# The way into a state-space loop: SiLU by exponential and logarithm, batches 0 to 2 ahead, TensorE's order written by hand

## The chip, the cores and the metric

The kernel runs as one program on one core of a Trainium2 chip. The metric is the device time of an execution in microseconds, from the first to the last instruction of the core. The engines are written as the profile writes them: PE is TensorE (PEld its weight loads), ACT is ScalarE, DVE is VectorE, POOL is GpSimd, SP the engine that issues DMAs. They run side by side and meet at semaphores. Each engine works through its own instructions in the order in which they are written.

## The reference

Two layers of a small network over `x` (4 batches, 128 tokens, 128 channels) and a context (4 batches, 2048 keys), all float32. The part that the change touches is the first layer's state-space branch and the two attentions on either side of it:

```python
x = x + L0_xattn(layernorm(x), ctx)      # attention over every 16th key, 16 heads of 8
x = x + L0_attn(layernorm(x))            # the state-space branch, below
...                                      # quantised feed-forward, gated attention over the context
x = x + L1_attn(layernorm(x))            # self-attention with a relative bias
...                                      # quantised feed-forward

xi, res = split(x @ W_in)                # 256 channels each
u = silu(conv4(xi) + conv_b)             # causal convolution with 4 taps
dbc = u @ W_x                            # 8 + 16 + 16 values of each token
delta = softplus(dbc[:8] @ W_dt + b_dt)
h = exp(delta * A) * h + delta * B * u   # over the tokens, for 16 states
y = (sum over states of h * C + u * D) * silu(res)
return y @ W_out
```

## The kernel before, in words

Channels or tokens lie on the 128 partitions, and the 512 tokens of the four batches along the free dimension. Every engine's program is written out by hand, so the order of the code is the order on the engine, and semaphores named after tensors (`S["u"]`, `S["dt_ps"]`) hold the engines together. A helper `mm` issues every matmul, so that most of PE's matmuls bear one line (L1076). A product in float32 shows as two matmul instructions in the trace.

Both attentions run through the function `attention(ph)`, which each engine has in its own version: `ph` 0 is the cross-attention of layer 0, `ph` 1 the self-attention of layer 1. Step `t` handles the scores of one batch and head group (16 in all, four for each batch), and the later stages of a batch `b` come due at step `4 * b + stage`, by a table of constants: INVERSE 6, INVERSE_T 7, VALUES 8 (`pv`, then `spread_ps`), SCALE 9 (DVE writes `attn_T`), PROJECT 10 (PE multiplies `attn_T`), ADD 11 (DVE makes the new `x` and its moments), RSTD 11, NORM 12, TURN 13. Within a step PE does: scores, the turned probabilities of step t-2, values and their scale, projection. DVE does: `neg_max` (the maximum of the scores), the copy of turned probabilities, `attn_T`, sum and moments, norm, reciprocal. ACT does the four exponentials, and then `o_T`, the copy of `pv`. The last steps (16 to 25) hold only the stages of batches 2 and 3.

After the cross-attention comes the way into the state loop. The convolution is folded into the input projection: for each of four taps one matmul with `w_tap` (the input weights times the tap) on a shifted view of `xn_pad`. The tokens are cut into three groups, batches 0 and 1, batch 2, batch 3 (`SSM_GROUPS`). `channels` issues the convolutions (`part` 0 and 1, the two halves of 128 channels) and the gate's product; the first group's are spread over steps 17 to 25 of the attention by the table `CHANNELS`. ACT takes SiLU of each straight out of PSUM (`channel_inputs`, `gates`). For that it loads the table set of SiLU before (L492), and the set of exponential and logarithm again behind (L528). Then for all 512 tokens at once: PE makes `dbc_ps`; ACT copies its first 8 rows (`dt_low`) and rounds 96 rows to bf16 (`bc_parts`); DVE takes the two remainders of that rounding (L862, L863), so that three bf16 parts stand for one float32 value; PE makes `dt_ps`; ACT takes the absolute value, exponential and logarithm (L532 to L536), DVE the positive part (L867); their sum is `delta` (L873), and `du` is `delta * u`, for the first half on DVE (L877), for the second on POOL (L384). During the remainders PE runs 16 matmuls on ones, whose result nobody reads (`keep_warm`).

The loop has 32 steps k, one for each state n and half. DVE makes `drive` (L884, `du` times the row of B that PE spreads over the partitions) and runs the scan (L900); ACT makes `decay` (L556) and copies the spread row of C; POOL multiplies the state by C (`read`, L392), and PE adds that up in PSUM (`y`) on top of the product with `skip`. Behind it DVE multiplies with the gate (L905). POOL quantises the weights of the feed-forwards in three instructions each (L375 to L377), the first three ahead of the loop, two behind.

## Time and profile before

| | |
|---|---|
| time, median of 3 runs | 279.73 us (277.42 to 280.04) |
| span of the profiled execution | 278.8 us |
| PE busy | 209.7 us (75%) |
| DVE busy | 205.7 us (74%) |
| ACT busy | 151.6 us (54%) |
| POOL busy | 74.6 us (27%) |
| table loads of ACT on the way in | 2, each 1.28 us |
| first scan of the state loop | 85.55 us from the start |

The profiled execution is one of its own, and only its span is given, no time beside it; the span lies between the lowest and the highest of the three runs. The busy shares are means over stages with different limits, so they don't say what a stage waits for: the rows further down, cut by stage, do.

### The profile page before, as it was taken

What the parts mean: (1) busy time and instruction counts of PE and PEld (TensorE: products, weight loads), DVE (VectorE), ACT (ScalarE), POOL (GpSimd) and SP (SyncE); (2) the same over time, 40 slices, a digit from 0 to 9 for tenths busy, and PEclk for the clock granted to TensorE, in tenths of its full rate; (3) what the DMA queues carried; (4) which work ended last, traced back from release to release, by engine and by line L of the source; (5) the groups of instructions that cost most, each with busy time, mean ns of one, the idle gap of its engine ahead of it and who ended that gap; (6) DMA issues with size and microseconds to landing.
All of it is one profiled execution on the core that took longest, in us unless ns stands there. A gap on an engine that the chain in (4) does not pass through costs nothing.

```text
span 278.8 us, 4790 instructions
## 1 busy us (share of the span) xinstructions
PE 209.7 (75%) x1557; PEld 141.2 (51%) x1559; DVE 205.7 (74%) x585; ACT 151.6 (54%) x510; POOL 74.6 (27%) x73
## 2 busy tenths in 40 slices
PE   6896988898786977777762577999996699973313
PEld 4475877676752322222131354777785688851102
DVE  6358648873069999999957975767767499985675
ACT  4357659643685555555317773245336689853420
POOL 5013000049305777777794010000001000001000
PEclk9688999999979799999996899999999899997555
DMA  7999700068830000000000005000000000000001
GB/s 225 429 393 414 317 2 2 0 74 93 94 45 0 1 0 1 0 0 0 2 1 0 1 0 150 2 0 2 0 1 0 4 1 2 0 4 0 4 0 38
DMA packets 6745, 16.06 MB, mean 58 GB/s; under 512 B 320, under 2 KB 5056, under 8 KB 5696
## 3 DMA queue, kind: packets, MB, share of 16 engines
q1 hardware_dynamic: 6720, 15.75, 19.7%
q8 instruction: 13, 0.21, 0.3%
q14 instruction: 12, 0.10, 0.1%
HBM read 13.39 MB, written 2.35 MB: 56 GB/s over the span
## 4 chain that ended last, share of the span: by engine, by line
PE 38%; DVE 24%; POOL 13%; issue 12%; ACT 9%; DMA 2%; POOLq 0%; SPq 0%; another core or an unknown queue 0%; DVEq 0%; ACTq 0%
PE bank L1076 31%; POOL region L392 13%; ACT probs L477 3%; PE bank L1416 3%; DVE region L775 2%; DVE region L758 2%; DMA ctx_T_sb<-ctx_T 2%; PE bank L1189 2%; DVE neg_max L753 1%; DVE xn L685 1%; DVE stats L680 1%; PE bank L1093 1%; DVE ext L1040 1%; DVE ext L1041 1%; DVE v_heads L698 1%
## 5 line engine op out<-in xcount | busy, mean ns | idle before, releaser
L1076 PE MATMUL bank<-region,early_sb 128*128 128x512 f32 x64 | 36.8, 661 | 11.8 <-POOL region L392 11.6
L392 POOL TENSOR_TENSOR region<-region 128x512 f32<-128x512 f32 x32 | 40.5, 1268 | 14.5 <-DVE region L900 14.5
L900 DVE TENSOR_TENSOR_SCAN region<-region,bank 128x512 f32<-128x512 f32 x32 | 38.7, 1211 | 0.0
L1076 PE MATMUL bank<-k_groups,region 128*128 128x128 f32 x256 | 35.7, 285 | 1.2 <-ACT k_groups L459 1.2
L1076 PEld LDWEIGHTS bank<-k_groups,region 128*128 128x128 f32 x256 | 32.2, 198 | 3.2 <-ACT k_groups L459 1.8
L361 POOL TENSOR_TENSOR xb<-x,rows_sb 128x512 f32<-128x512 f32 x3 | 3.8, 1261 | 101.0 <-DVE x L790 43.2
L477 ACT ACTIVATE probs<-bank,neg_max 128x128 f32<-128x128 f32 x64 | 22.6, 367 | 12.9 <-DVE neg_max L753 12.5
L1076 PE MATMUL bank<-ctx_T_sb,region 128*32 128x128 f32 (+1 forms) x288 | 26.8, 345 | 3.4 <-DMA ctx_T_sb<-ctx_T 2.2
L477 ACT ACTIVATE probs<-region,neg_max 128x128 f32<-128x128 f32 x64 | 24.9, 390 | 5.7 <-DVE neg_max L758 5.5
L1076 PEld LDWEIGHTS bank<-region,early_sb 128*128 128x128 f32 x64 | 10.1, 195 | 33.2 <-POOL region L392 32.6
L775 DVE COPY region<-bank 128x512 f32<-128x512 f32 x32 | 21.8, 682 | 5.6 <-PE bank L1189 5.6
L411 ACT ACTIVATE lnv<-mv,eps_col 128x1 f32<-128x1 f32 x24 | 7.0, 291 | 33.7 <-DVE mv L681 33.6
L542 ACT ACTIVATE region<-bank 128x512 f32<-128x512 f32 x16 | 9.5, 595 | 24.2 <-POOL region L392 24.2
L1189 PE MATMUL bank<-early_sb,probs 128*128 128x128 f32 x128 | 20.7, 287 | 1.5 <-ACT probs L477 1.5
L884 DVE TENSOR_TENSOR bank<-region,bank 128x512 f32<-128x512 f32 x32 | 21.6, 676 | 0.0
L556 ACT ACTIVATE region<-region,a_neg 128x508 f32<-128x508 f32 x32 | 21.1, 708 | 0.0
L758 DVE CUSTOM_DVE_ANT_0 region<-bank,region 128x128 f32<-128x128 f32 x64 | 14.5, 282 | 5.7 <-PE bank L1076 5.7
L1189 PEld LDWEIGHTS bank<-early_sb,probs 128*128 128x128 f32 x128 | 15.2, 146 | 3.5 <-ACT probs L477 2.1
L1007 DVE COPY region<-bank 128x512 f32<-128x512 f32 x16 | 10.9, 686 | 8.1 <-PE bank L1416 8.1
L1076 PEld LDWEIGHTS bank<-region,ctx_sb 128*128 128x128 f32 x128 | 15.4, 192 | 2.9 <-issue 2.9
L1076 PEld LDWEIGHTS bank<-ctx_T_sb,region 128*32 128x32 f32 (+1 forms) x288 | 12.6, 132 | 7.7 <-issue 4.5
L1076 PE MATMUL bank<-region,ctx_sb 128*128 128x128 f32 x128 | 15.6, 275 | 0.0
(198 smaller groups left out, 410.1 us busy)
## 6 DMA issues: line engine op xcount, KB each, us to landing
ctx_sb<-ctx SPq DMA_DIRECT2D x4, 1024.0 KB, 24.5
ctx_T_sb<-ctx_T SPq DMA_DIRECT2D x3, 1024.0 KB, 10.5
late_sb<-late SPq DMA_DIRECT2D x1, 2416.0 KB, 18.4
bias_scratch<-bias_vec SPq DMA_DIRECT2D x1, 2040.0 KB, 24.7
ctx_T_sb<-ctx_T SPq DMA_DIRECT2D x2, 512.0 KB, 6.2
region<-bias_scratch SPq DMA_DIRECT2D x1, 1024.0 KB, 5.7
early_sb<-early SPq DMA_DIRECT2D x1, 512.0 KB, 3.7
region<-taps SPq DMA_DIRECT2D x1, 512.0 KB, 18.9
```

The lines of the kernel that those rows point to most:

```text
L392: done(pool.tensor_tensor(read[:, k % 3, :], state[:, k % 3, :], c_sb[:, n % 2, :], ALU.mult), "read")
L477: ins = act.activation(probs[:, w % 4, j, :], src[:, j, :], ACT.Exp, bias=neg_max[:, w % 4, j:j + 1], scale=1.0 if ph == 0 else -1.0, accu ...
L542: done(act.activation(c_sb[:, n % 2, :], bank[2][:, :], ACT.Copy), "c_sb")
L556: done(act.activation(dst, src, ACT.Exp, scale=a_neg[:, hf, n:n + 1]), "decay")
L758: ins = dve.tensor_tensor_reduce(neg_biased[:, t % 3, j, :], src[:, j, :], rel_bias[:, HG * g + j, :], -1.0, HIGHEST, ALU.add, ALU.min, ne ...
L775: done(dve.tensor_copy(probs_T[:, w % (2 * NG)].rearrange("p h k -> p (h k)"), bank[3 + w % 2][:, :]), "probs_T_sb")
L884: done(dve.tensor_tensor(bank[3 + k % 3][:, :], du[:, hf, :], bank[n % 2][:, :], ALU.mult), "drive")
L900: done(dve.tensor_tensor_scan(state[:, k % 3, :], decay[:, k % NDA, :], bank[3 + k % 3][:, :], 0.0, ALU.mult, ALU.add), "state")
L1007: done(dve.tensor_copy(p2_T[:, w % 4].rearrange("p c q -> p (c q)"), bank[4 + w % 2][:, :]), "p2T_sb")
L1076: return pe.matmul(dst, lhsT, rhs, start=start, stop=stop)
L1189: ins = pe.transpose(bank[3 + w % 2][:, j * P:j * P + P], probs[:, w % 4, j, :], ident)
L1416: ins = pe.transpose(bank[4 + w % 2][:, c * P:c * P + P], p2[:, b % 2, g, c * P:c * P + P], ident)
```

## The change

- `u` and the gate no longer use the SiLU table. DVE takes the convolution with its bias from PSUM, clamped at -80, into `du` (`clamped`), and ACT makes the sigmoid in three steps of one table set, exp(-x), ln(1 + that), exp(-that) (`sigmoids`); POOL (pieces 0 and 1) and DVE (piece 2) multiply. Both table loads go.
- The gate is only clamped on the way in (two halves for batches 0 to 2, one for batch 3). Its six sigmoid steps stand in the state loop on ACT, at k = 6, 8, ... 16, and DVE multiplies them in behind the last scan.
- What was done for 512 tokens at once is done in pieces: `dbc`, the low rank copy, the remainders, `dt_ps`, the logarithm and `delta` for batches 0 to 2 (384 columns, first half), then for batch 3 (128 columns, both halves), then batches 0 to 2 of the second half. The positive part and the sum are one instruction (`stepped`), and the bias has one of its own (`biased`).
- The attention's loop ends at step 16 for `ph` 0, and the rest is written by hand on PE, ACT and DVE with the convolutions between. The copies of the turned `xn` of batches 2 and 3 move from ACT to DVE.
- The table of stages changes for both attentions: PROJECT 10 to 9, ADD and RSTD 11 to 10, NORM 12 to 11; in a step DVE writes `attn_T` ahead of the copy of turned probabilities.
- The 16 matmuls on ones go. The third weight of POOL is quantised behind the loop. `skip` is made at the start. The last `x` shares its memory with the third.

```diff
-INVERSE, INVERSE_T, VALUES, SCALE, PROJECT, ADD, RSTD, NORM, TURN = 6, 7, 8, 9, 10, 11, 11, 12, 13
+INVERSE, INVERSE_T, VALUES, SCALE, PROJECT, ADD, RSTD, NORM, TURN = 6, 7, 8, 9, 9, 10, 10, 11, 13
+STEPS = 4 * NB, NG * (NB - 1) + NORM + 1
-FILLS = {"early_in": 20, "bc_parts": 16, "hidden": 12, "hidden_rest": 12, "swiglu_out": 4}
+FILLS = {"early_in": 20, "hidden": 12, "hidden_rest": 12, "swiglu_out": 4}
+PIECES = [(0, 2), (2, 3), (3, 4)]
+FIRST = 3 * P
+GATE_STEPS = (6, 8, 10, 12, 14, 16)
...
# ACT
+            copy_xn_T(1, 1)
+            heads_out(2)
+            rsqrt_var(1, 2)
+            heads_out(3)
+            rsqrt_var(1, 3)
+            sigmoids(0)
+            sigmoids(1)
+            sigmoids(2)
+            low_rank(0, 3, slice(0, FIRST))
+            log_terms(0, slice(0, 1), slice(0, FIRST))
+            low_rank(1, 4, slice(FIRST, T))
+            log_terms(1, slice(0, DH), slice(FIRST, T))
+            log_terms(2, slice(1, 2), slice(0, FIRST))
...
+            def log_terms(i, hfs, cols):
+                act.wait_ge(S["dt_sum"], i + 1)
+                link(act.activation(sp[:, hfs, cols], delta[:, hfs, cols], ACT.Abs))
+                link(act.activation(sp[:, hfs, cols], sp[:, hfs, cols], ACT.Exp, scale=-1.0))
+                done(act.activation(sp[:, hfs, cols], sp[:, hfs, cols], ACT.Ln, bias=1.0), "sp_exp")
...
# DVE
+            clamped(2)
...
+            done(dve.tensor_tensor(u[:, :, piece(2)], du[:, :, piece(2)], sig[:, :, piece(2)], ALU.mult), "u_last")
+            split(0, 3, slice(0, FIRST))
+            biased(0, 1, slice(0, 1), slice(0, FIRST))
+            split(1, 4, slice(FIRST, T))
+            biased(1, 6, slice(0, DH), slice(FIRST, T))
+            stepped(0, slice(0, 1), slice(0, FIRST))
...
+            stepped(1, slice(0, DH), slice(FIRST, T))
...
+            biased(2, 2, slice(1, 2), slice(0, FIRST))
...
             drive(0)
+            stepped(2, slice(1, 2), slice(0, FIRST))
...
# PE
+            project(0, 3)
+            convolve(0, 1, range(2, CONV))
+            turn_xn(1, 1, 2)
+            convolve(1, 0)
+            convolve(1, 1)
+            turn_xn(1, 1, 3)
+            pe.wait_ge(S["attn"], 4)
+            gates(0, 0, 3, bank[5][:, 0:FIRST])
+            done(gates(1, 0, 3, bank[7][:, 0:FIRST]), "gates_ps")
+            convolve(2, 0)
+            convolve(2, 1)
+            gates(0, 3, 4, bank[0][:, 2 * P:3 * P])
+            done(gates(1, 3, 4, bank[0][:, 3 * P:4 * P]), "gates_ps")
```

ACT between the last SiLU and the first decay of the loop. Before, it stands so:

```order
L451 ACTIVATE region<-bank 128x2x128
L524 ACTIVATE region<-early_sb,cols_sb 128x128 x2
L526 ACTIVATE region<-bank 8x512
L527 ACTIVATE bc_parts<-bank 96x512
L528 ACT_TABLE_LOAD
L532 ACTIVATE region<-bank,cols_sb 128x512 x2
L535 ACTIVATE region<-region 128x512
L536 ACTIVATE region<-region 128x512
```

In the changed kernel, from the last step of the last sigmoid (three more logarithm steps on 384 columns follow ahead of the first decay):

```order
L456 ACTIVATE region<-region 128x2x128
L462 ACTIVATE region<-bank 8x384
L463 ACTIVATE bc_parts<-bank 96x384
L468 ACTIVATE region<-region 128x384
L469 ACTIVATE region<-region 128x384
L470 ACTIVATE region<-region 128x384
L462 ACTIVATE region<-bank 8x128
L463 ACTIVATE bc_parts<-bank 96x128
L468 ACTIVATE region<-region 128x2x128
L469 ACTIVATE region<-region 128x2x128
L470 ACTIVATE region<-region 128x2x128
```

One pair of copies and one set of logarithm steps has become two pairs and three sets, which alternate; the second pair of copies (L462, L463 on 128 columns) stands behind the first set's logarithm.

DVE at the same place. Before:

```order
L862 TENSOR_TENSOR region<-bank,bc_parts 64x512
L863 CAST bc_parts<-region 64x512
L862 TENSOR_TENSOR region<-region,bc_parts 32x512
L863 CAST bc_parts<-region 32x512
L867 TENSOR_SCALAR region<-bank,cols_sb 128x512 x2
L873 TENSOR_TENSOR region<-region 128x512
L877 TENSOR_TENSOR region<-region 128x512
```

In the changed kernel:

```order
L908 TENSOR_TENSOR region<-bank,bc_parts 64x384
L909 CAST bc_parts<-region 64x384
L908 TENSOR_TENSOR region<-region,bc_parts 32x384
L909 CAST bc_parts<-region 32x384
L918 TENSOR_SCALAR region<-bank,cols_sb 128x384
L908 TENSOR_TENSOR region<-bank,bc_parts 64x128
L909 CAST bc_parts<-region 64x128
L908 TENSOR_TENSOR region<-region,bc_parts 32x128
L909 CAST bc_parts<-region 32x128
L918 TENSOR_SCALAR region<-bank,cols_sb 128x128 x2
L925 SCALAR_TENSOR_TENSOR region<-region 128x384
L959 TENSOR_TENSOR region<-region 128x384
```

The remainders and the bias come once for 384 and once for 128 columns, and the first `delta` (L925) stands behind both.

PE in the self-attention, from the values of batch 0 on. Before:

```order
L1076 MATMUL bank5<-region,v_heads 32x128 x16
L1076 MATMUL bank7<-inv_T,cols_sb 128x128
L1076 MATMUL bank0<-k_groups,region 128x128 x4
L1189 MATMUL bank4<-early_sb,probs 128x128 x4
L1076 MATMUL bank1<-k_groups,region 128x128 x4
L1189 MATMUL bank3<-early_sb,probs 128x128 x4
L1076 MATMUL bank5<-late_sb,attn_T 128x128
L1076 MATMUL bank2<-k_groups,region 128x128 x4
```

In the changed kernel:

```order
L1166 MATMUL bank5<-region,v_heads 32x128 x16
L1166 MATMUL bank7<-inv_T,cols_sb 128x128
L1166 MATMUL bank0<-k_groups,region 128x128 x4
L1254 MATMUL bank4<-early_sb,probs 128x128 x4
L1166 MATMUL bank5<-late_sb,attn_T 128x128
L1166 MATMUL bank1<-k_groups,region 128x128 x4
L1254 MATMUL bank3<-early_sb,probs 128x128 x4
L1166 MATMUL bank2<-k_groups,region 128x128 x4
```

The projection of `attn_T` has moved ahead of the scores of step 10 (those into bank1) and of the turned probabilities behind them.

## Rows read from the trace of the kernel before

**Rows 1.** The page: shares of the chain by line.

```profile
PE bank L1076 31%; POOL region L392 13%; ACT probs L477 3%; PE bank L1416 3%; DVE region L775 2%; DVE region L758 2%; DMA ctx_T_sb<-ctx_T 2%; PE bank L1189 2%; DVE neg_max L753 1%; DVE xn L685 1%; DVE stats L680 1%; PE bank L1093 1%; DVE ext L1040 1%; DVE ext L1041 1%; DVE v_heads L698 1%
```

**Rows 2.** Windows: stretch, us; busy PE, PEld, DVE, ACT, POOL; PE clock; DMA, GB/s.

```profile
57.40:74.90 17.50, 15.77 (x150) 13.20 (x150) 6.28 (x22) 9.21 (x31) 12.38 (x9) 1.00 0.84 93
...
78.90:85.50 6.60, 6.10 (x25) 3.31 (x24) 6.27 (x10) 6.50 (x12) 0.63 (x1) 0.74 0.12 16
85.50:139.70 54.20, 42.49 (x92) 12.66 (x90) 54.17 (x64) 27.07 (x46) 39.68 (x32) 0.97 0.00 1
222.60:249.80 27.20, 24.74 (x261) 21.33 (x259) 25.92 (x152) 22.98 (x111) 0.00 (x0) 0.98 0.01 2
```

**Rows 3.** The chain of waits in order of time, 57 to 90 us.

```profile
69.89 5.00 PE bank L1076 x41
74.89 1.84 issue
...
82.76 0.70 DVE region L873
```

**Rows 4.** Timeline, ACT on the way in: start, us, instruction, idle before.

```profile
69.13 1.28 ACT L492 ACT_TABLE_LOAD   x1
...
70.59 0.83 ACT L444 ACTIVATE region<-bank,cols_sb 128x256 f32<-128x256 f32 x2
...
78.92 1.28 ACT L528 ACT_TABLE_LOAD   x1
...
81.37 0.63 ACT L535 ACTIVATE region<-region 128x512 f32<-128x512 f32 x1
...
83.75 0.70 ACT L556 ACTIVATE region<-region,a_neg 128x508 f32<-128x508 f32 x1
```

**Rows 5.** Timeline, DVE from the remainders to the first scans.

```profile
78.94 0.68 DVE L862 TENSOR_TENSOR region<-bank,bc_parts 64x512 f32<-64x512 f32 x1 [9.43 <-ACT bc_parts L527]
...
79.65 0.42 DVE L863 CAST bc_parts<-region 64x512 bf16<-64x512 f32 x1
...
85.55 1.22 DVE L900 TENSOR_TENSOR_SCAN region<-region,bank 128x512 f32<-128x512 f32 x1
...
87.86 1.21 DVE L900 TENSOR_TENSOR_SCAN region<-region,bank 128x512 f32<-128x512 f32 x1
```

**Rows 6.** Timeline: a convolution on PE, POOL's product, PE's skip products.

```profile
60.84 3.72 PE L1076 MATMUL bank<-region 128*128 128x256 f32 x16 [0.37 <-ACT region L419]
...
84.87 1.27 POOL L384 TENSOR_TENSOR region<-region 128x512 f32<-128x512 f32 x1 [12.55 <-DVE region L873]
...
85.22 1.88 PE L1076 MATMUL bank<-region 128*128 128x512 f32 x4
```

**Rows 7.** Windows of one us: columns as in rows 2, granted PE clock third from last.

```profile
82.00:83.00 1.00, 1.00 (x7) 0.67 (x6) 0.92 (x3) 0.97 (x2) 0.00 (x0) 0.50 0.00 0
...
84.00:85.00 1.00, 0.50 (x4) 0.02 (x2) 0.96 (x3) 1.00 (x3) 0.13 (x1) 1.00 0.00 0
...
91.00:92.00 1.00, 1.00 (x2) 0.15 (x1) 1.00 (x2) 1.00 (x3) 1.00 (x1) 0.50 0.00 0
```

**Rows 8.** Timeline, DVE: the last two scans and the gate's product.

```profile
137.41 2.33 DVE L900 TENSOR_TENSOR_SCAN region<-region,bank 128x512 f32<-128x512 f32 x2
...
141.25 0.69 DVE L905 TENSOR_TENSOR region<-bank,region 128x512 f32<-128x512 f32 x1 [1.52 <-PE bank L1076]
```

**Rows 9.** Timeline of the self-attention, engine by engine: PE, ACT, then DVE.

```profile
233.63 1.06 PE L1076 MATMUL bank<-k_groups,region 128*128 128x128 f32 x8
...
234.10 0.28 ACT L488 ACTIVATE o_T<-bank 128x128 f32<-128x128 f32 x1
...
235.04 0.28 DVE L758 CUSTOM_DVE_ANT_0 region<-bank,region 128x128 f32<-128x128 f32 x1
...
242.81 0.29 DVE L758 CUSTOM_DVE_ANT_0 region<-bank,region 128x128 f32<-128x128 f32 x1
...
252.90 0.29 DVE L790 TENSOR_TENSOR x<-bank,xb 128x128 f32<-128x128 f32 x1 [0.58 <-PE bank L1076]
```

More of the change, by code:

```diff
@@ L455, in self_keys, with heads_out @@
+            def heads_out(v):
+                act.wait_ge(S["pv"], v + 1)
+                if v >= 1:
+                    act.wait_ge(S["attn"], v)
+                done(act.activation(o_T[:, :], bank[5][:, 0:P], ACT.Copy), "o_sb")
             def self_keys(b):
@@ L509, in _ @@
             values(0)
+            for hf in range(DH):
+                done(act.activation(skip[:, hf, :], ident, ACT.Copy, scale=C("d_skip", hf)), "skip")
             done(act.activation(one_hot_b[:, :], C("one_hot", 0, BC), ACT.Copy), "consts")
@@ L549, in _ @@
                 if n == 0:
[L550 removed]
+                    act.wait_ge(S["delta"], hf + 2)
                 if k >= NDA:
@@ new lines, in clamped, with split @@
+            def clamped(i):
+                dve.wait_ge(S["conv_ps"], DH * (i + 1))
+                if i == 2:
+                    dve.wait_ge(S["gates_ps"], 2)
+                for hf in range(DH):
+                    ins = dve.tensor_scalar(du[:, hf, piece(i)], conv_at(i, hf), C("conv_b", hf), LEAST, ALU.add, ALU.max)
+                done(ins, "xc")
+            def split(i, at, cols):
+                n = cols.stop - cols.start
+                dve.wait_ge(S["bc_hi"], i + 1)
+                for rest, end in ((bank[at][:, 0:n], 2 * BC), (bc_rest[:, cols], BC)):
+                    link(dve.tensor_tensor(bc_rest[0:end, cols], rest[0:end, :], bc_parts[0:end, cols], ALU.subtract))
+                    done(dve.tensor_copy(bc_parts[0:end, cols], bc_rest[0:end, cols]), "bc_parts")
+                    dve.wait_ge(S["bc_parts"], 2 * i + (1 if end > BC else 2))
```

392 lines of the change are left out of this document (217 added, 175 removed).

## The prediction

> **What bounds the kernel now.** I read the page's shares of the chain first: PE's matmuls carry 31% of it, POOL's loop products 13%, everything else a few per cent each [rows 1]. No engine bounds the whole, so I cut the span at the stages that the change touches and read the windows [rows 2]. From 57.4 to 74.9 us, the end of the cross-attention with the convolutions, PE is busy 15.8 of 17.5 us. From 78.9 to 85.5 DVE is busy 6.27 of 6.60 and ACT 6.50. In the state loop DVE is busy 54.17 of 54.20. In the self-attention (222.6 to 249.8) DVE is busy 25.9 of 27.2. The reader should see that DVE is full in three of four stages: what shortens ACT alone buys nothing there, and what makes DVE wait is paid in full. The loop starts with the scan at 85.55 and keeps its pace from the second at 87.86 [rows 5], so the way in is worth exactly what it moves these two.
>
> All durations come from the profiled execution, whose span is 278.8; the median of the runs is 279.73. I add the sum to both: a difference is the same for both, the forecast is for the median.
>
> **The way in, step by step.** *Sizes.* ACT takes 0.63 for 512 columns and 0.83 for two of 256 [rows 4], 0.28 for 128 [rows 9]; so 0.42 for 256 and, between, 0.52 for 384. DVE takes 0.68 for 512 columns and 0.42 for a cast [rows 5], 0.29 for 128 [rows 9]; so 0.42 for 256, 0.55 for 384, and 0.35 and 0.22 for casts of 384 and 128 (estimates by shape). A hop between engines costs 0.02 to 0.06, the gaps between the rows.
>
> *The two table loads* take 1.28 each on ACT [rows 4]. Neither is worth its length. During the first PE has the convolutions to run: the chain goes from 69.89 through 5.00 us of PE [rows 3]. After the second ACT and DVE reach the first `delta` (82.76) together, and DVE has been busy without a pause since 78.94 [rows 3, 5]. I cost both at a gain of 0, at most 0.7.
>
> *PE up to the last gate.* The products stay (a convolution of two batches and both halves is 3.72 [rows 6]), in other pieces. Without any wait they would end at 57.4 + 15.8 = 73.2; before they end at 74.9 [rows 2, 3]. Following the new order I find waits for the turned `xn` of batch 1, for the reciprocal and the projection of batch 3, and 0.5 us saved over all: PE ends at 74.4.
>
> *From there to the first scan* the changed kernel hands work to and fro, because each engine's order mixes the pieces: DVE clamps batch 3, two of 128 columns (0.6, to 75.0); ACT's three sigmoid steps on 256 (1.3, to 76.3), and only then its copies for batches 0 to 2 (two of 384, 1.0, to 77.3); DVE's remainders on 384 with their hops (1.9) and the bias (0.6, to 79.8), for which ACT waits; ACT's three logarithm steps on 384 (1.6, to 81.4), behind which stand the copies for batch 3 (0.5, to 81.9), for which DVE waits; DVE's remainders on 128 (1.1) and two biases (0.5, to 83.5), for which ACT waits; three logarithm steps on 256 (1.35, to 84.85); DVE's `delta`, `du` and the bias of the last piece (0.42 + 0.42 + 0.55, to 86.25), for which ACT waits again; three steps on 384 (1.6, to 87.85); the first decay, which ACT has behind them (0.70 [rows 4], to 88.55). The first scan starts at 88.6 instead of 85.55: **3.0 us later**. The second follows 2.3 behind the first, as before, since POOL's product is shorter than it was (1.27 for 512 [rows 6], about 0.96 for 384).
>
> *Cross-check by DVE's work.* From the moment when the copies are there (77.3) DVE has remainders 1.9 and 1.1, biases 0.6, 0.5 and 0.55, `delta` 0.55, 0.42 and 0.55, `du` 0.55 and 0.42, a drive 0.68: 7.8 us. Before it was 6.6 from 78.9. Even if no engine waited for another, the scan would start at 85.1: the work done ahead is eaten by the smaller pieces. That is the bound on the other side, a gain of 0.4; with PE ending at 73.2 instead of 74.4 it is a gain of 1.6.
>
> *What lies beside other work.* POOL multiplies `u` for batches 0 to 2 from about 71.3, where its third weight stood: 1.27 for 512 columns [rows 6] and 0.7 for 256, done at 73.5, ahead of PE's 74.4. ACT makes `skip` (two of 0.28) at the start, where it waits for the first maxima. The exponentials' table set is then never left on the way in. All this I cost at nothing; if POOL's cover were gone, 0.7.
>
> *PE's clock.* The 16 matmuls on ones go. The granted clock was 0.50 (1.2 GHz) at 82 to 83, behind the stretch from 74.9 on in which PE had waited 1.84 us and more, and 1.00 (2.4 GHz) at 84, with PE busy 6.10 of the 6.60 us from 78.9; it was 0.50 again at 91 to 92 inside the loop [rows 2, 3, 7]. In the changed kernel PE has single products between 78 and 88.6 and will start the loop at 1.2 GHz. The skip products, 1.88 at the higher clock [rows 6], then take 1.8 more ahead of the first `y`. Before, 3.4 us at the low clock inside the loop held up no scan. I take 0.3, with 0 and 2.0 as ends.
>
> [...]
>
> "ScalarE: Activation LUTs" of the Trainium skill, section "What ACT_TABLE_LOAD costs", gives about 2.66 us for a switch, 1.28 of load and 1.38 of drain. The rows have only the load: the first ends at 70.41, and by 70.59 ACT has begun a SiLU [rows 4], which leaves no room for 1.38. By the page two switches would free 5.3 us of ACT instead of 2.6, and if all of that were on the path the way in would be 2.3 us shorter rather than 3.0 longer.
>
> **The loop and its end.** Six sigmoid steps of 0.63 on ACT lie in a stage where it is busy 27.1 of 54.2 us [rows 2]: nothing. If the cover were gone they would cost 3.8. The two gate products of DVE, 2 x 0.69, fall in its idle 1.52 us before L905 [rows 8]: nothing, at most 0.2. POOL's third weight moves behind the loop, ahead of the other two; the layer that reads it has its own norm and first products to do before, so nothing.
>
> **The self-attention** gets the new table too. The projection now stands ahead of the scores of step 10, and waits for `attn_T`. DVE makes that behind `neg_max` of step 9, once `o_T` is there at 234.38 [rows 9]: 234.65. The projection takes 0.4, the scores start at 235.05 instead of 233.63, take 1.06 and end at 236.1. DVE began `neg_max` of step 10 at 235.04 [rows 9]: it stands idle and is 1.05 late. In step 13 the same comes back larger: the sum, moments and norm have moved ahead, `neg_max` of step 12 ends at 241.6, four exponentials (4 x 0.39) and `o_T` follow to 243.5, `attn_T` 0.25, projection 0.35, scores 1.06, so that `neg_max` of step 14 starts at 245.2 instead of 242.81 [rows 9]. Behind step 16 there are no scores to delay. DVE is full throughout, so nothing gives it back: the sum of batch 3 moves from 252.90 to 255.3, **2.4 us later**. Ends: 0.3 (the reordering of the tail gives most back) and 2.8. The cross-attention has the same table, but there keys and values of the next batch (PE) lie between the scores and the projection, and `attn_T` is ready in time: 0, within 0.3.
>
> **Sum:** 3.0 + 0.3 + 2.4 = 5.7. The profile's span goes from 278.8 to 284.5, the median from 279.73 to 285.4.
>
> **Rivals.** *Only one of the two places costs* (the other's waits close, because `o_T` or the copies come earlier than I read): 2.4 to 3.3, so 282.1 to 283.0. For it speaks that each is a chain of ten estimates; against it, that DVE is full in both stages [rows 2].
> *Nothing to be measured:* the way in nets out as in the cross-check and the self-attention loses under 1.0: 279.3 to 281.
> *Faster:* the low-rank copies for batches 0 to 2 get in early. This needs ACT's copies by 74.3 rather than 77.3, so that the remainders lie beside PE's last convolution: PE would have to lose the 1.84 us of "issue" that stand on the chain at 74.89 [rows 3] and its waits besides. Then the scan starts 3 us ahead of now, at 82.5, and the kernel takes 276.7 with a self-attention unchanged. The decision falls at the end of ACT's copies: before 74.3 it is a gain, after 77 not.
> *The clock decides too:* the `y` products at 1.2 GHz fall behind the loop's pace, 54.2 / 32 = 1.7 a step [rows 2], for some steps: 2.0 instead of 0.3, 287.1.
>
> **Chances.** Forecast (within 1.5 of 285.4) 0.50; one place only 0.22; nothing 0.13; faster 0.07; clock too 0.08. About 1% (2.8 us) is what a measurement of this kernel can tell from no change. Slower than 282.5: 0.50 + 0.08 + 0.13 of the second case = 0.71; within 1%: 0.22; faster than 276.9: 0.07. The range from 279.6 to 288.5 holds the forecast, the clock and most of the second and third case.
>
> **What the new profile would show.** First scan at 88.6, second at 90.9; DVE idle about 2 us between its first biases and the second remainders, and ACT idle three times ahead of an absolute value; granted clock 0.50 when the loop starts; the loop's pace unchanged; DVE idle 0.8 us ahead of `neg_max` of step 10 in the self-attention, with PE's projection as releaser of the wait. I am wrong if ACT's copies for batches 0 to 2 end before 76, or if that idle time in the self-attention doesn't appear.

## The result and the profile after

The changed kernel takes 290.99 us (median of 4, 289.71 to 291.65) against 279.88 of the kernel before beside it: ratio 1.044, 95% interval 1.038 to 1.051. That is 11 us slower; the forecast was 5.7 slower, and 290.99 lies above the range, which ended at 288.5. The profiled execution took 290.91 us with a span of 289.0, which is 10.2 more than the span before. Some executions of a kernel are over 1.5% above its fastest one: the ratios leave these out, the medians and ranges have them.

I read the trace at anchors that both kernels have. Each line is the distance between two starts, and the last column is what the prediction gave it.

| stretch | before | after | differs | forecast |
|---|---|---|---|---|
| start to the last maximum of the cross-attention | 56.65 | 56.46 | -0.2 | 0 |
| from there to the first scan | 28.90 | 32.07 | +3.2 | +3.0 |
| first to fourth scan | 5.73 | 6.27 | +0.5 | +0.3 |
| fourth to last but one scan | 46.13 | 46.12 | 0 | 0 |
| from there to the first `x` behind the loop | 6.27 | 6.97 | +0.7 | 0 |
| from there to the feed-forward's first sum | 18.90 | 19.93 | +1.0 | 0 |
| from there to the first maximum of the self-attention | 49.63 | 51.04 | +1.4 | 0 |
| from there to the sum of batch 3 | 40.69 | 44.31 | +3.6 | +2.4 |
| from there to the end | 25.90 | 25.83 | -0.1 | 0 |

**The way in.** ACT first, from the copies of batches 0 to 2 to the first decay (start, us, instruction, idle time before it and who ended it):

```profile
75.73 0.48 ACT L462 ACTIVATE region<-bank 8x384 f32<-8x384 f32 x1
76.24 0.49 ACT L463 ACTIVATE bc_parts<-bank 96x384 bf16<-96x384 f32 x1
79.34 0.52 ACT L468 ACTIVATE region<-region 128x384 f32<-128x384 f32 x1 [2.61 <-DVE region L918]
...
83.37 0.42 ACT L468 ACTIVATE region<-region 128x256 f32<-128x256 f32 x1 [1.81 <-DVE region L918]
...
86.17 0.52 ACT L468 ACTIVATE region<-region 128x384 f32<-128x384 f32 x1 [1.48 <-DVE region L918]
...
87.70 0.70 ACT L569 ACTIVATE region<-region,a_neg 128x508 f32<-128x508 f32 x1
```

DVE in the same stretch:

```profile
76.76 0.55 DVE L908 TENSOR_TENSOR region<-bank,bc_parts 64x384 f32<-64x384 f32 x1 [0.59 <-ACT bc_parts L463]
...
81.60 0.28 DVE L908 TENSOR_TENSOR region<-bank,bc_parts 64x128 f32<-64x128 f32 x1 [2.29 <-ACT bc_parts L463]
...
87.83 0.56 DVE L925 SCALAR_TENSOR_TENSOR region<-region 128x384 f32<-128x384 f32 x1 [1.10 <-ACT region L470]
88.53 1.22 DVE L987 TENSOR_TENSOR_SCAN region<-region,bank 128x512 f32<-128x512 f32 x1
...
90.85 1.21 DVE L987 TENSOR_TENSOR_SCAN region<-region,bank 128x512 f32<-128x512 f32 x1
```

The reader should see two engines that take turns: ACT idle three times ahead of its absolute value, each time released by DVE's bias, and DVE idle 2.29 us ahead of its second remainders, released by ACT's copy. Where DVE had no pause from 78.94 on before [rows 5], it now has pauses of 2.29, 0.32 and 1.10 us (the 0.32 stands ahead of the second `delta`, in a row not shown).

**PE's clock at the loop's start** (windows; columns as in rows 2) and the four skip products with it:

```profile
85.50:90.00 4.50, 1.29 (x3) 0.39 (x4) 3.26 (x6) 3.09 (x6) 1.16 (x2) 0.50 0.00 0
...
88.50:143.20 54.70, 44.21 (x95) 13.44 (x95) 54.24 (x64) 31.90 (x53) 40.13 (x32) 0.95 0.00 0
```

```profile
90.14 3.62 PE L1166 MATMUL bank<-region,skip 128*128 128x512 f32 x4
```

They took 1.88 before [rows 6]. The fourth scan is 0.5 late for it, and then the pace holds: DVE is busy 54.24 of 54.70 us.

**The loop's end.** The timeline of DVE and of POOL behind the last scan:

```profile
143.16 2.53 DVE L991 TENSOR_TENSOR region<-region 128x512 f32<-128x512 f32 x2
145.72 1.33 DVE L995 TENSOR_TENSOR region<-bank,region 128x512 f32<-128x512 f32 x2
...
147.89 0.29 DVE L998 TENSOR_TENSOR x<-bank,x 128x128 f32<-128x128 f32 x1 [0.84 <-PE bank L1166]
```

```profile
142.21 2.93 POOL L408 TENSOR_TENSOR region<-region 128x512 f32<-128x512 f32 x2 [0.44 <-DVE region L987]
```

The two gate products (L991) take 1.26 us each. A DVE product of this size with both operands in SBUF took 0.70 in the kernel before, while POOL was idle (L873 [rows 3]). They lie on top of POOL's last two reads, which take 2.93 for two (2.48 before). The product with the gate begins 2.5 us behind the last scan instead of 1.5 [rows 8].

**The quantisation of `xn`** behind the loop, DVE and then POOL:

```profile
153.72 0.53 DVE L1010 TENSOR_SCALAR q_step<-q_abs 128x2 f32<-128x2 f32 x1
...
154.48 0.56 DVE L1018 TENSOR_SCALAR q_mul<-q_inv 128x2 f32<-128x2 f32 x1
...
155.08 0.67 DVE L1029 TENSOR_SCALAR q_up<-q_step,w_scale 128x4 f32<-128x4 f32 x1
155.78 0.63 DVE L1032 TENSOR_SCALAR xq<-region 128x128 bf16<-128x128 f32 x4
```

```profile
152.73 1.49 POOL L391 TENSOR_SCALAR wq_w1T<-w_tmp 128x512 bf16<-128x512 f32 x1
154.32 0.69 POOL L389 TENSOR_SCALAR w_tmp<-late_sb,w_inv 128x512 f32<-128x512 f32 x1
155.10 1.95 POOL L390 TENSOR_SCALAR w_tmp<-w_tmp 128x512 f32<-128x512 f32 x1
```

`q_mul` has two numbers on each partition and takes 0.56 us, where it took 0.17 before; it ends at 155.04, POOL's L389 at 155.01. `q_up` takes 0.67 instead of 0.22. `q_step` ends at 154.25, POOL's L391 at 154.22, but it is no loss of the change: it took 0.53 before as well, with POOL beside it. With the third weight behind the loop too, POOL is still quantising here; before it was done at 149.82. The 1.0 us from the first `x` to `xq` is 0.39 of `q_mul`, 0.44 of `q_up` and 0.19 in the norm ahead of them.

**The self-attention**, step 10: DVE's `attn_T` and maximum, PE's projection between them.

```profile
240.94 0.29 DVE L771 TENSOR_TENSOR attn_T<-o_T,bank 128x128 f32<-128x128 f32 x1
...
242.71 0.29 DVE L813 CUSTOM_DVE_ANT_0 region<-bank,region 128x128 f32<-128x128 f32 x1 [0.87 <-PE bank L1166]
```

```profile
241.29 0.49 PE L1166 MATMUL bank<-late_sb,attn_T 128*128 128x128 f32 x2 [0.97 <-DVE attn_T L771]
241.61 1.06 PE L1166 MATMUL bank<-k_groups,region 128*128 128x128 f32 x8
```

The maximum of step 10 is 7.67 us later than before, and that of step 9 was 6.53 later: 1.1 us, in the place and by the wait that the prediction names. Counted from the first maximum, that of step 14 comes at 33.16 instead of 30.60, 2.6 us late where the prediction has 2.4, and that of step 15 at 35.51 instead of 32.20, 3.3 late. The tail (steps 18 to 21) has something the prediction doesn't name:

```profile
258.63 0.28 DVE L777 TENSOR_TENSOR x<-bank,xb 128x128 f32<-128x128 f32 x1
258.95 0.29 DVE L702 BATCH_NORM_STATS2 stats<-x 128x6 f32<-128x128 f32 x1
259.27 0.18 DVE L703 BATCH_NORM_AGGREGATE mv<-stats 128x2 f32<-128x6 f32 x1
259.37 0.23 DVE L784 RECIPROCAL inv_sum<-row_sum 128x16 f32<-128x16 f32 x1
...
263.17 0.29 DVE L777 TENSOR_TENSOR x<-bank,xb 128x128 f32<-128x128 f32 x1 [0.89 <-PE bank L1166]
```

```profile
256.91 0.48 PE L1166 MATMUL bank<-inv_T,cols_sb 16*128 16x128 f32 x2 [0.55 <-DVE inv_T L790]
...
259.66 0.28 PE L1286 MATMUL bank<-early_sb,inv_sum 128*16 128x128 f32 x1 [1.34 <-DVE inv_sum L784]
```

The reciprocal of batch 3 (L784) now stands behind the sum and the moments of batch 2, in one step; PE waits 1.34 us for it. The copy of the turned reciprocal (L790) stands behind the norm and the extremes in the same way (0.55). From the maximum of step 15 to the sum of batch 3 it takes 8.80 us; before it took 8.49.

### The profile page after: what moved, and what is told of

Same layout as the page of the kernel before. It is cut to its first block and busy times, and to the rows that moved or that the text cites. A ratio compares the mean times of both kernels' runs of the same rounds, so it can differ in the third digit from the quotient of the medians.

```text
span 289.0 us, 4803 instructions
## 1 busy us (share of the span) xinstructions
PE 212.7 (74%) x1543; PEld 141.3 (49%) x1543; DVE 214.8 (74%) x607; ACT 154.8 (54%) x517; POOL 77.4 (27%) x75
## 5 line engine op out<-in xcount | busy, mean ns | idle before, releaser
L408 POOL TENSOR_TENSOR region<-region 128x512 f32<-128x512 f32 x32 | 41.1, 1285 | 14.5 <-DVE region L987 13.6
L1166 PE MATMUL bank<-region,early_sb 128*128 128x512 f32 x64 | 35.5, 640 | 11.1 <-POOL region L408 11.1
L1166 PE MATMUL bank<-k_groups,region 128*128 128x128 f32 x256 | 36.7, 291 | 1.2 <-ACT k_groups L482 1.2
L1166 PEld LDWEIGHTS bank<-k_groups,region 128*128 128x128 f32 x256 | 33.1, 203 | 3.4 <-ACT k_groups L482 1.8
L569 ACT ACTIVATE region<-region,a_neg 128x508 f32<-128x508 f32 x32 | 21.8, 709 | 0.1
L808 DVE TENSOR_REDUCE neg_max<-bank 128x4 f32<-128x512 f32 x16 | 10.9, 684 | 6.5 <-PE bank L1166 6.4
```

The source lines that it names most:

```text
L408: done(pool.tensor_tensor(read[:, k % 3, :], state[:, k % 3, :], c_sb[:, n % 2, :], ALU.mult), "read")
L569: done(act.activation(dst, src, ACT.Exp, scale=a_neg[:, hf, n:n + 1]), "decay")
L808: done(dve.tensor_reduce(neg_max[:, w % 4, :], src, AX, ALU.max, negate=True), "neg_max")
L1166: return pe.matmul(dst, lhsT, rhs, start=start, stop=stop)
```

## The experiments

Four of the kernels ran once, with the profile: the gate products on POOL, both with matmuls on ones, and the one with two edits in the self-attention. One ran twelve times, the others four times. The changed kernel did not run again beside them, and the medians of the kernel before were 279.86, 281.51 and 280.98 us in the three rounds, so a difference of medians to the changed kernel is good to a microsecond or two.

The distances between two anchors of one trace tell more, and each has its own scatter. The way in takes 32.07, 32.09, 32.08, 32.09, 32.09, 32.08 and 32.07 us in the seven profiles that have its orders unedited and the convolutions at full clock, and this although the granted clock fell in some of them at 76 us and in the changed kernel only behind 80; in the kernel before it took 28.90, and 27.94 in another profile of the same code. From the last but one scan to the first `x` it is 6.96 or 6.97 wherever the gate products stand behind the loop, and 6.26 or 6.27 elsewhere. From there to the feed-forward's first sum it is 19.58 to 19.93 in the nine profiles with the third weight behind the loop, and 18.90 to 19.10 in the four with it ahead. From the first maximum of the self-attention to the sum of batch 3 it is 43.85 to 45.73 in the seven profiles with the new table unedited, and 40.69 and 40.70 in the two with the old one.

### The way in: one pair of instructions exchanged

ACT's list; the second run has both edits, the second of them on DVE.

```diff
+            low_rank(1, 4, slice(FIRST, T))
             log_terms(0, slice(0, 1), slice(0, FIRST))
-            low_rank(1, 4, slice(FIRST, T))
             log_terms(1, slice(0, DH), slice(FIRST, T))
# the second run, DVE, also:
             biased(1, 6, slice(0, DH), slice(FIRST, T))
+            biased(2, 2, slice(1, 2), slice(0, FIRST))
             stepped(0, slice(0, 1), slice(0, FIRST))
...
-            biased(2, 2, slice(1, 2), slice(0, FIRST))
```

> One edit in the changed kernel: ACT copies the low rank rows of batch 3 ahead of the logarithm steps for batches 0 to 2, not behind them. The theory that the way in is late by waits handed to and fro: PE has the product for batch 3 at about 77.8, so the copies end at 78.4, DVE takes its second remainders behind its first bias at 79.3 instead of 81.6, its two biases are there by 81, ACT's second logarithm set ends at 82.4 and the last one, behind DVE's bias at 83.8, at 85.5; first scan near 86.2 instead of 88.5, the kernel 2.3 us shorter (288.7). The rival, that the smaller pieces are simply more work: the same instructions run, so the first scan stays within 0.5 us of 88.5 and the time does not move.

Measured: three executions of 287.36, 287.94 and 288.88 us, 3 us under the changed kernel, ratio to the kernel before 1.029 (1.022 to 1.037). The fourth, the profiled one, took 663 us with PE busy for 629 of them, for no reason that a row shows; it is left out, and no distance is read from its trace. So the first scan near 86.2 stays unchecked for this edit alone.

> Two edits in the changed kernel, both in the order alone: ACT copies the low rank rows of batch 3 ahead of the logarithm steps for batches 0 to 2, and DVE takes the last bias (384 columns of the second half) ahead of the first delta, not behind du of batch 3. The theory of waits handed to and fro: ACT's third logarithm set starts behind its second, near 82.5, instead of 86.17, and the stretch from the last maximum of the cross-attention to the first scan shrinks from 32.1 us to between 28 and 29, the kernel by 3.5 to 4 (287 to 287.5). The rival (more work in smaller pieces) leaves the stretch within 0.5 of 32.1.

Measured: 288.88 us (285.38 to 290.91), ratio 1.023 (1.004 to 1.042). The distance from the last maximum to the first scan is 29.57, 2.5 us less than 32.08: the same instructions in another order, so the rival of "more work" falls. It still misses the 28 to 29 expected, and the time misses its 287 to 287.5. PE's rows give a reason for the distance: dropped to 1.2 GHz by 78, it makes the low rank products in 2.57 us, which took 1.52 in the changed kernel.

```profile
77.83 2.57 PE L1166 MATMUL bank<-region,late_sb 8*128 8x384 f32 x6 [1.88 <-ACT region L462]
```

### Matmuls on ones again

The first run has 16 of them, in the changed kernel as it stands; the second has 12, 4 and 12 with the two edits of order.

```diff
                      "b_ps")
+                if n == 0:
+                    keep_warm(16, 7)
# the second run: 12 there, and
             done(state_inputs(1, bank[3][0:DBC, 2 * P:FIRST]), "dbc_ps")
...
+            keep_warm(12, 7)
...
             done(state_inputs(2, bank[4][0:DBC, 0:P]), "dbc_ps")
+            keep_warm(4, 7)
```

> One look. The changed kernel with 16 matmuls on ones again, between PE's first spread row of B and the first of C, where PE is idle for 4 us. The theory that PE enters the loop at 1.2 GHz because it had nothing to do before: the granted clock is 1.00 by 89, the four skip products take 1.9 us instead of 3.6, and the fourth scan comes 0.5 us earlier against the first (5.8 instead of 6.3). The rival, that PE's clock falls there whatever it did: 0.50 from 88 to 90 as in the changed kernel, the fourth scan at 6.3.

```profile
85.31 3.61 PE L1166 MATMUL bank<-ones 128*128 128x256 bf16 x16
...
90.92 1.88 PE L1166 MATMUL bank<-region,skip 128*128 128x512 f32 x4
```

The skip products are back at 1.88 and the fourth scan at 5.73 behind the first, as before the change: 0.5 us, as expected. The execution as a whole took 292.33. PE had been at 1.2 GHz in the convolutions (granted clock 0.50 from 60 to 64), where the other profiles but one have 1.00; that cost it 2.7 us between the last maximum and the clamp of batch 3 (20.0 instead of 17.3).

> One look. The changed kernel with the two edits of order in the way in (as in the earlier run, whose stretch from the last maximum of the cross-attention to the first scan was 29.57), and 12, 4 and 12 matmuls on ones where PE is idle: behind the first low rank product, behind that of batch 3, and behind the first spread row. The theory that the mended order fell short of 28 to 29 because PE had dropped to 1.2 GHz by 78 and made the low rank products in 2.57 us instead of 1.52: stretch 28.5, clock 1.00 from 78 to 84, the fourth scan 5.73 behind the first. The rival, that matmuls on ones delay the products behind them as much as the clock gives: 29.5 or more.

```profile
73.50:78.00 4.50, 4.50 (x29) 2.82 (x26) 2.94 (x7) 2.35 (x7) 0.00 (x0) 1.00 0.82 91
78.00:83.00 5.00, 3.27 (x14) 1.80 (x13) 4.76 (x13) 4.79 (x10) 0.00 (x0) 0.66 0.08 13
```

```profile
83.16 1.22 DVE L987 TENSOR_TENSOR_SCAN region<-region,bank 128x512 f32<-128x512 f32 x1
```

The clock is 1.00 up to 78, the low rank products take 1.52 again, DVE is busy 4.76 of the 5.00 us from 78, and the distance to the first scan is 28.11 us (expected 28.5; 28.90 before the change, 27.94 in another profile of the same code). It fell to 0.66 from 78 to 83, where 1.00 was expected, at no visible cost. From the end of ACT's copies to the first scan it is 7.84 us, where the changed kernel has 11.80: that is the 7.8 of DVE's own work in the prediction's cross-check. So the way in is 3.2 us longer by its waits, behind which PE's lower clock is hidden; without them that clock costs 1.5 (29.57 against 28.11), and with both mended nothing is lost. The one execution took 284.79 us, 6.2 under the changed kernel; 1.4 of that is the feed-forward's stretch, which no edit touched and which ran at full clock here.

### The loop's end: the gate products moved to POOL

```diff
# POOL, in the loop
+                if k in (20, 24):
+                    hf = (k - 20) // 4
...
+                    done(pool.tensor_tensor(gate[:, hf, :], gate[:, hf, :], gate_s[:, hf, :], ALU.mult), "gated")
# DVE, behind the loop
-                ins = dve.tensor_tensor(gate[:, hf, :], gate[:, hf, :], gate_s[:, hf, :], ALU.mult)
```

> One look. The changed kernel with the two gate products moved from DVE behind the last scan to POOL inside the state loop (behind its reads of steps 20 and 24). The theory that DVE and POOL slow each other when both read and write SBUF alone behind the last scan: POOL's last two reads take 2.5 us instead of 2.93, the product with the gate starts 1.5 us after the last scan's end instead of 2.5, the first x of the loop's layer comes 0.7 us earlier against the last scan (5.1 instead of 5.8 from its start), and no scan is late. The rival, that the two products cost by their own work on DVE alone (2 x 0.69 with an idle time of 1.5 to lie in): they cost nothing and the distance stays 5.8.

```profile
145.05 0.69 DVE L996 TENSOR_TENSOR region<-bank,region 128x512 f32<-128x512 f32 x1 [1.52 <-PE bank L1167]
```

```profile
126.66 1.26 POOL L412 TENSOR_TENSOR region<-region 128x512 f32<-128x512 f32 x1
127.88 2.49 POOL L408 TENSOR_TENSOR region<-region 128x512 f32<-128x512 f32 x2
...
142.50 2.48 POOL L408 TENSOR_TENSOR region<-region 128x512 f32<-128x512 f32 x2 [0.44 <-DVE region L991]
```

POOL's last reads take 2.48 again, the idle time of 1.52 is back, and the first `x` comes 6.26 us behind the last but one scan (6.27 before, 6.97 changed). No scan is late: from first to last but one 52.42 (52.39). The 0.7 us belong to the gate products beside POOL's reads. The one execution took 291.29 us: a gain of 0.7 is under what one time can show.

### The third weight ahead of the loop again

```diff
             quantise_weight(1)
+            quantise_weight(2)
...
-            for i in (2, 3, 4):
+            for i in (3, 4):
```

> The changed kernel with POOL's third weight quantised ahead of the state loop again, in front of the two products for u. If POOL's weights behind the loop are what slows the quantisation of xn on DVE, q_up takes 0.22 again instead of 0.67 and the first PE product of the feed-forward comes 1.0 us earlier after the loop; and if the 1.4 us lost before the last norm of the feed-forward is only PE's clock in another phase, it may come or go, so the kernel is 1.0 to 2.4 us shorter (288.6 to 290). POOL's third weight ends near 71, the products for u start then and PE waits for them not at all. The rival, that the weight has to be out of the way before the loop: the u products come late and the first scan moves from 88.5 to 89.5, and nothing is gained.

```profile
153.03 0.17 DVE L1019 TENSOR_SCALAR q_mul<-q_inv 128x2 f32<-128x2 f32 x1
...
153.24 0.22 DVE L1030 TENSOR_SCALAR q_up<-q_step,w_scale 128x4 f32<-128x4 f32 x1
```

```profile
151.28 1.49 POOL L391 TENSOR_SCALAR wq_w2T<-w_tmp 128x512 bf16<-128x512 f32 x1
```

POOL is done at 152.77, `q_mul` takes 0.17 and `q_up` 0.22 again, and the distance from `x` to the feed-forward's first sum goes from 19.93 to 19.10: 0.8 of the 1.0. What is left is the 0.19 in the norm, where POOL still quantises beside DVE. With the scatter of both groups of profiles (19.58 to 19.93, 18.90 to 19.10) the third weight's place is worth 0.5 to 1.0. The way in keeps its 32.08, so the rival falls. But the time is 292.69 us (289.93 to 293.85), no shorter: in the next stretch, up to the self-attention, the profile lost 1.8 us more than the changed kernel, and 1.4 more up to the sum of batch 3 in the self-attention. The windows of that stretch, of the kernel before, this one, and the one with the matmuls on ones in the way in:

```profile
162.58:212.21 49.63, 44.75 (x290) 33.78 (x288) 34.36 (x90) 20.51 (x69) 2.52 (x2) 1.00 0.08 22
```

```profile
165.53:218.34 52.81, 48.09 (x296) 35.53 (x294) 34.47 (x91) 20.54 (x69) 2.53 (x2) 0.95 0.08 21
```

```profile
161.74:211.38 49.64, 44.75 (x290) 33.78 (x288) 34.35 (x90) 20.52 (x69) 2.52 (x2) 1.00 0.08 22
```

The change edits nothing in this stretch. Where the granted clock is 1.00 from 3 us ahead of it to its end, it takes 49.63 and 49.64; in the eleven other profiles parts are below and it takes 50.46 (the kernel before with the new table, whose code up to there is the kernel before) to 52.81. In the changed kernel it is 51.04, where PE is at 1.2 GHz in the second half of the feed-forward:

```profile
166.56 2.71 PE L1166 MATMUL bank<-ones 128*128 128x256 bf16 x12
169.10 0.61 PE L1460 MATMUL bank<-ident_b,region 128*128 128x128 bf16 x8
```

Those twelve took 1.47 before, and the turned hidden values (L1460) wait for them. So the +1.4 goes with PE's clock and with no instruction of this stretch. Of the changed kernel and its variants ten profiles of eleven have the lower clock there, and of the code before one of two: whether the change makes it more frequent is not shown. At 3.2 us it is the largest difference that unedited code shows between these profiles.

### The self-attention's table, undone and done alone

The old table in the changed kernel for this attention alone, and the new one in the kernel before.

```diff
# the changed kernel, ph 1 one step later
-                    if due(t, PROJECT) is not None:
+                    if due(t - ph, PROJECT) is not None:
# and the same for ADD, RSTD, NORM; attn_T behind the turned probabilities
# the kernel before, ph 1 one step earlier
-                    if due(t, PROJECT) is not None:
+                    if due(t + ph, PROJECT) is not None:
# and the same for ADD, RSTD, NORM; attn_T ahead of the turned probabilities
```

> The changed kernel with the old table of stages in the self-attention alone (projection in step 10 behind the scores, sum one step later, norm one step later, attn_T behind the turned probabilities). If the table is what makes the self-attention longer, the stretch from its first maximum (neg_max) to the sum of batch 3 goes back from 34.0 to 30.2 us and the kernel is 3.7 us shorter (287.3). If the stretch is longer because everything arrives in another phase of PE's clock, the stretch stays above 33 and the time within 1 us of 291.

Measured: 286.32 us (285.14 to 288.44), 4.7 under the changed kernel; ratio 1.024 (1.016 to 1.032). From the first maximum to the sum of batch 3 it takes 40.70 us, and the kernel before 40.69.

> The kernel before with one part of the change alone: the new table of stages in the self-attention (projection in step 9 ahead of the scores of step 10, sum and norm one step earlier, attn_T ahead of the turned probabilities). The table theory: 3.7 us longer than the kernel before (283.6), with DVE idle 1 us before the maximum of step 10 and the sum of batch 3 at 256.6. My blind sum for this part, 2.4, would give 282.3. The theory that the phase of PE's clock made it longer: within 1 us of the kernel before.

Measured: 285.43 us (285.19 to 285.51), ratio 1.020 (1.014 to 1.026), 5.6 above the kernel before. The stretch is 45.27 us. The table alone costs 3.6 in the changed kernel and 4.6 in this profile; in both directions it is the table that decides. The size goes with the clock: of the profiles with the new table, those with a granted clock of 1.00 in the second half of the stretch take 43.9 to 44.2, the changed kernel with 0.93 takes 44.3, and those with 0.91 or 0.92, this one among them, 45.3 to 45.7. With the old table it is 40.69 at 0.93 and 40.70 at 0.86.

### The table's cost in two parts

```diff
# first run, PE: the projection alone
-                    if due(t, PROJECT) is not None:
+                    if due(t - ph, PROJECT) is not None:
# second run, DVE, in ph 1: the reciprocal alone (the third run has both)
+                    inverse(...) and inverse_turned(...), where due
                     if due(t, ADD) is not None:
                         added(ph, due(t, ADD))
                     if due(t, NORM) is not None:
                         normed(i_out, due(t, NORM))
-                    inverse(...) and inverse_turned(...), where due
```

> The changed kernel with the projection alone put back to step 10 behind the scores in the self-attention; sum, norm and attn_T keep the new places. It splits the table's cost (3.6 to 4.9 us in the three profiles so far, from the first maximum of the self-attention to the last sum of the kernel). If the projection ahead of the scores is all of it, as my blind sum had it, the stretch is 62.9 us again instead of 66.4 and the kernel 3.6 shorter. If the sum and norm, one step earlier on DVE, carry a part, the stretch lies between 64 and 65.5. If the sum in the same step as the projection makes DVE wait for PE, the stretch stays at 66 or grows.

Measured: 290.03 us (289.30 to 290.48), ratio 1.032 (1.027 to 1.036). The stretch to the last sum of the kernel is 64.98 instead of 66.44, to the sum of batch 3 it is 42.84 instead of 44.31: 1.5 us less, not all of it. The cut between projection and the rest is not clean here, because PE's clock was lower in the tail: the values of batch 3 took 1.89 us, and 1.08 in the changed kernel.

```profile
256.61 1.89 PE L1166 MATMUL bank<-region,v_heads 128*32 128x128 f32 x32
```

Up to the sum of batch 2, ahead of these, it is 37.71 us instead of 39.77: 2.1 us.

> The changed kernel with one order changed in the self-attention on DVE: the reciprocal of the next batch's row sums and the copy of its turned form come ahead of the sum, the moments and the norm of this batch within a step, not behind them. The table itself stays as changed. The theory: by moving sum and norm one step up, the table put them in front of the reciprocal and its copy, for which PE waits (1.34 and 0.55 us ahead of the last batch), and that is the 2.1 us that the projection's place does not explain. From the first maximum to the sum of batch 3 the stretch is then 42.2 us instead of 44.31, the kernel 2.1 shorter (289). The rival, that DVE is full there and its order gives nothing: 44.3 and no change. A third, that the earlier sum and norm push the maxima out: 43.5 to 44.3.

Measured: 289.13 us (287.81 to 290.43), ratio 1.030 (1.025 to 1.036). The stretch is 42.47 us: 1.8 shorter, of 2.1 expected. Only 0.2 of it is there at the maximum of step 15; the rest lies in the tail, which takes 7.14 us instead of 8.80.

> One look. The changed kernel with both edits of the self-attention: the projection back in step 10 behind the scores, and the reciprocal with its copy ahead of sum and norm. If the two causes are separate and make up the whole of it, the stretch from the first maximum to the sum of batch 3 is 44.31 - 1.47 - 2.1 = 40.7, as in the kernel before (40.69). If they overlap, 41.5 to 42.5. If the earlier sum and norm are then a gain, under 40.5.

```profile
256.81 0.24 DVE L784 RECIPROCAL inv_sum<-row_sum 128x16 f32<-128x16 f32 x1
256.98 0.23 DVE L777 TENSOR_TENSOR x<-bank,xb 128x128 f32<-128x128 f32 x1
...
259.98 0.29 DVE L777 TENSOR_TENSOR x<-bank,xb 128x128 f32<-128x128 f32 x1 [0.58 <-PE bank L1172]
```

```profile
257.11 0.28 PE L1292 MATMUL bank<-early_sb,inv_sum 128*16 128x128 f32 x1 [0.45 <-DVE inv_sum L784]
```

The reciprocal stands ahead of the sum, PE waits 0.45 us for it instead of 1.34, and the sum of batch 3 comes 40.64 us behind the first maximum: the kernel before has 40.69. The one execution took 287.65 us. The two causes make up the whole: 1.8 us by the reciprocal (44.31 to 42.47), and 1.8 by the projection once the reciprocal is ahead (42.47 to 40.64), both in profiles with nearly the same clock. The earlier sum and norm, which this kernel keeps, cost 1.3 us in the maxima (that of step 15 at 33.50 instead of 32.20) and give them back in the tail (7.14 instead of 8.49).

### Everything mended

> The changed kernel with everything mended that the runs so far showed: the two edits of order and the matmuls on ones in the way in (-3.5, and -0.55 in the loop), the gate products on POOL inside the loop (-0.7), the third weight ahead of the loop (-0.8), the projection back in step 10 and the reciprocal ahead of sum and norm in the self-attention (-3.6). By the ledger 291.0 - 9.2 = 281.8, within 2 of the kernel before, with PE's clock in the feed-forward as what is left (0 to 3). If the parts do not add up because a later stage takes back what an earlier one gives, above 285. If the work done ahead is then a gain at last, under 279.

Measured: 281.34 us (median of 12, 278.42 to 283.80) against 280.98 of the kernel before beside it; ratio 1.000, interval 0.996 to 1.004. That is near the 281.8 of the ledger and no gain. The ledger had 1.9 above the kernel before, measured is 0.4; the agreement to half a microsecond in the time itself is in part luck, since the kernel before was 1.1 slower in this round. In its profile the way in took 30.83 us, for PE's clock fell in the convolutions there (20.0 us from the last maximum to the clamp instead of 17.3, as with the 16 matmuls on ones); from the clamp to the first scan it is 10.81, as in the mended way in above. No version beat the kernel before, and the two removed table loads gained nothing that shows. No run takes the loads out alone.

## Why the prediction was wrong in size

It had the direction, and 10.1 us in the profile stand against a sum of 5.7. Of its three terms the first two were near and the third too small by 1.2: the step that failed there is "DVE is full throughout, so nothing gives it back" and "behind step 16 there are no scores to delay", which leave out that the reciprocal now stands behind the sum. Three further terms that it set to nothing cost 3.1 us.

- **The way in, +3.0 by waits handed to and fro:** right, +3.2, and by the waits named. The chain's points held within 0.7 us (copies done at 76.73, forecast 77.3; first scan 88.53, forecast 88.6). That the last one fits to 0.1 is luck: the start was forecast 0.6 late, and the way from the copies to the scan, 11.8 us, was forecast as 11.3. Two exchanges of order gave back 2.5. The cross-check by DVE's work has 7.8 us from the copies on, and 7.84 were measured without waits. Against the other profile of the old code (27.94) the term is 4.1.
- **Table loads, a gain of 0:** nothing speaks against it. With waits and clock mended the way in is 28.11, and that of the kernel before 28.90 and 27.94; but the mended one also has more and smaller pieces, so what the loads alone are worth is not shown.
- **PE's clock at the loop's start, +0.3:** +0.5. The price stood between its ends and was mis-sized by little.
- **"At most 0.2" for the two gate products in the idle 1.52:** wrong, +0.7. The step priced them at 0.69 each, from rows where one operand is in PSUM [rows 5, 8]. These have both in SBUF, which by itself costs nothing (0.70 with POOL idle [rows 3]), but POOL reads SBUF beside them: 1.26 each. The Trainium skill, "SBUF — State Buffer", section "Who interferes with whom", says that a DVE instruction with two SBUF inputs contends with a GpSimd instruction that reads SBUF; the 1.26 and POOL's 2.93 for 2.48 agree.
- **POOL's third weight, "so nothing":** wrong, +1.0 in this profile, 0.5 to 1.0 over all. The step asked only when the weight is needed, and not what POOL's work would lie beside. It lies beside DVE's smallest instructions. The same section of the Trainium skill says of a DVE instruction in one of the 2-port modes, which a `tensor_scalar` can take, and a GpSimd instruction that whoever issues first has the shared pair for the whole instruction and the other blocks. `q_step` and `q_mul` agree, ending 0.03 us behind POOL's; `q_up`, which ends at 155.75 while POOL's instruction beside it runs to 157.05, does not.
- **The self-attention, +2.4:** right in place and in size up to step 14 (+1.1 in step 10, forecast 1.05; +2.6 in step 14, forecast 2.4), too small in the sum, +3.6. The projection ahead of the scores, on which the whole term rested, is worth 1.8 to 2.1. What the step missed is that sum and norm moved ahead of the next batch's reciprocal and its copy: 1.8. "Behind step 16 there are no scores to delay" was true, but PE waits there for the reciprocal (1.34 us), and that took 1.7 us of the tail. Without it the earlier sums would have given 1.3 back there, which is what the lower end of the term (0.3, "the reordering of the tail gives most back") had in mind.
- **The rest of the kernel, nothing:** +1.4 in the feed-forward, which goes with PE's clock. No step had it, since the clock was weighed only where the change removed matmuls. What sets the clock there stays open.
- **The cross-attention, within 0.3:** -0.2 in this profile. It shows little: the last maximum comes at 54.66 to 57.42 us in the eleven profiles with this code.

## What to carry to other kernels

When a whole is cut into pieces for an earlier start, write down for each engine what stands in front of the piece that another engine waits for; two exchanges of order gave 2.5 us back, while taking out two table loads gained nothing that shows. When an item in a table of stages moves, look at everything that it now stands in front of, and not only at its own inputs. And before work is laid into idle time at nothing, look at what the other of DVE and POOL does in that time, and where the operands lie.

## What the runs showed of the hardware

- Two DVE products with both operands in SBUF took 2.53 us beside POOL's SBUF product, against 0.70 for one with POOL idle, while in the loop DVE's scans (one operand in PSUM) kept 1.21 us beside the same POOL instruction.
- DVE instructions on two or four numbers a partition (`q_mul`, `q_up`) took 0.38 to 0.67 us beside POOL's quantisation, and 0.17 and 0.22 without it.
- Of PE's clock: the same code in the same stretch, entered at other times, ran at 1.00 or below and took 49.63 to 52.81 us; in two of eleven profiles with the changed kernel's code there, the clock was 0.50 in the convolutions behind the cross-attention, which cost 2.7 us. In the last kernel it was 0.50 from 82 to 90 us, behind 6 us in which PE had been busy throughout and 0.9 of idle time; in the kernel with both edits of order and the matmuls on ones, whose instructions there are the same, it was back at 1.00 by 83. What decides it stays open.
- One execution of the first experiment took 663 us with the granted clock at 1.00 throughout. Its cause stays open.
